# Attention sums of a graph network kernel: numerators scaled from SBUF, small products in one PSUM bank and earlier in TensorE's order, six banks of sums added four tiles late

## What is computed

```python
h = (x @ W).reshape(num_nodes, H, C)
a_src = (h * att_src).sum(-1)
a_dst = (h * att_dst).sum(-1)
e = jax.nn.leaky_relu(a_src[src] + a_dst[dst], NEG_SLOPE)
m = jax.ops.segment_max(e, dst, num_segments=num_nodes)
ex = jnp.exp(e - m[dst])
denom = jax.ops.segment_sum(ex, dst, num_segments=num_nodes)
alpha = ex / denom[dst]
out = jax.ops.segment_sum(alpha[:, :, None] * h[src], dst, num_segments=num_nodes)
```

## Time and profile before

| | |
|---|---|
| median of 3 runs | 11274.33 us (11269.1 to 11277.22) |
| span of the profiled execution | 11269.5 us |
| first attention sum, first to last tile on TensorE | 6399.8 to 7944.4 us |
| second attention sum | 8037.7 to 9565.7 us |
| busy share of the span | PE 66%, DVE 54%, ACT 29%, POOL 59% |

### The profile page before, as it was taken

How to read it: one execution, slowest core, us unless ns; L and a number is a source line. 1 busy time by engine, 2 the same in 40 slices (tenths; PEclk the granted TensorE clock), 3 DMA queues, 4 the chain that set the end, 5 groups by cost and what they waited for, 6 DMA issues and landing times. The chain is left out here.

```text
span 11269.5 us, 163779 instructions
## 1 busy us (share of the span) xinstructions
PE 7444.9 (66%) x37173; PEld 5482.0 (49%) x37173; DVE 6117.7 (54%) x21451; ACT 3221.2 (29%) x10474; POOL 6628.6 (59%) x7026
## 2 busy tenths in 40 slices
PE   4444444443466677578888666677577677788888
PEld 3222223333324555434434455556566566777777
DVE  5555544333324555455544466566566666677777
ACT  1111110000011111000000244444344444677776
POOL 4666666666644666656666466666466664555554
PEclk5566655555568888655555566666666666999999
DMA  3222223111143111111111122222122221211111
GB/s 89 69 77 77 72 79 80 46 46 46 44 163 128 44 44 44 44 48 45 46 46 46 45 48 48 48 48 49 44 48 49 49 49 38 79 41 41 41 41 40
DMA packets 297939, 639.01 MB, mean 57 GB/s; under 512 B 125149, under 2 KB 165984, under 8 KB 285534
## 3 DMA queue, kind: packets, MB, share of 16 engines
q0 software_dynamic: 223872, 420.21, 15.3%
q1 hardware_dynamic: 73470, 212.61, 5.6%
HBM read 479.52 MB, written 152.84 MB: 56 GB/s over the span
## 5 line engine op out<-in xcount | busy, mean ns | idle before, releaser
L1313 POOL DMA_INDIRECT relsum_rows<-relation_table,tab_idx x1870 | 1764.0, 943 | 1176.4 <-issue 463.6
L1364 PE MATMUL relsum_sums<-relsum_hot,relsum_rows 128*128 128x128 f32 x3740 | 950.2, 399 | 1055.2 <-issue 513.2
L1364 PEld LDWEIGHTS relsum_sums<-relsum_hot,relsum_rows 128*128 128x128 f32 x3740 | 782.6, 268 | 1274.5 <-issue 1239.1
L1097 POOL DMA_INDIRECT conv_rows<-tensor_table,src_idx x997 | 939.9, 943 | 754.3 <-PE conv_sums L2482 352.1
L1097 POOL DMA_INDIRECT gat1sum_rows<-gat_table,src_idx x997 | 941.2, 944 | 600.5 <-PE gat1sum_sums L2093 277.6
L1097 POOL DMA_INDIRECT gat2sum_rows<-gat_table,src_idx x997 | 942.2, 945 | 587.8 <-PE gat2sum_sums L2093 307.1
L1313 POOL DMA_INDIRECT gcnsum_rows<-x_table,src_idx x997 | 943.8, 947 | 553.2 <-issue 247.0
L727 POOL DMA_INDIRECT records<-sort_recs,place_rows x968 | 926.8, 957 | 581.5 <-DVE place_rows L234 303.7
L1323 DVE TENSOR_SCALAR relsum_hot<-relsum_digits,dst_rel,w 128x128 f32<-128x128 f32 x1994 | 803.3, 403 | 411.4 <-issue 410.8
L2091 PE MATMUL gat1sum_sums<-gat1sum_hot,gat1sum_scaled 128*128 128x128 f32 x1994 | 678.5, 439 | 421.8 <-DVE gat1sum_scaled L2020 367.0
L2091 PE MATMUL gat2sum_sums<-gat2sum_hot,gat2sum_scaled 128*128 128x128 f32 x1994 | 668.3, 434 | 426.2 <-DVE gat2sum_scaled L2020 300.5
(11 more groups left out here) (436 smaller groups left out, 16112.1 us busy)
## 6 DMA issues: line engine op xcount, KB each, us to landing
relation_table<-table_row SPq DMA_DIRECT2D x30, 2048.0 KB
relation_table<-sort_space SPq DMA_DIRECT2D x40, 1024.0 KB
place_lo_wide<-lo_rows SPq DMA_DIRECT2D x121, 256.0 KB
relsum_rows<-relation_table,tab_idx POOLq DMA_INDIRECT x1870
relation_table<-place_extra SPq DMA_DIRECT2D x20, 1024.0 KB
gcnsum_rows<-x_table,src_idx POOLq DMA_INDIRECT x997
gat1sum_rows<-gat_table,src_idx POOLq DMA_INDIRECT x997
gat2sum_rows<-gat_table,src_idx POOLq DMA_INDIRECT x997
```

What stands on the lines that cost most here:

```text
L1097: pool.indirect_dma_start(bufs[:, t % depth, :], None, table, bass.IndirectOffsetOnAxis(ap=idx[:, t:t + 1], axis=0)).then_inc(landed[t % l ...
L1313: pool.indirect_dma_start(rows[:, t % depth, :], None, table, bass.IndirectOffsetOnAxis(ap=idx[:, t:t + 1], axis=0)).then_inc(landed[t % d ...
L1364: mm = pe.matmul(bank[:, 0:P], part, hot[:, t % HOTS, :], start=k == 0, stop=k == len(tile_rows) - 1)
```

## The change

`LEAD` = 4 and `LANES` = 6 are new. The sums get six banks, and VectorE adds the sums of the tile four before, where it was two before; `scaled` has six buffers; the list of window starts is padded by 4. The numerators are transposed into the bank of the small products, not into three banks of their own, and VectorE scales rows from the SBUF copy `p_col`, which now has three copies. On TensorE the fold moves from tile 6 to tile 3, the spread from 8 to 5, the numerators from 12 to 9, and the transposes of the scores from tile 0, for the next group, to tile 12, for the group after the next. Group 1 is transposed ahead of the first tile.

```diff
+LEAD = 4
+LANES = 6
...
-        p_col = sb("p_col", [P, P], F32)
+        p_col = sb("p_col", [P, PHASES, P], F32)
...
-        scaled = sb("scaled", [P, 4, HEADS, CH], F32)
+        scaled = sb("scaled", [P, LANES, HEADS, CH], F32)
...
-        p_ps = [ps(f"p{f}", [P, 512], F32) for f in range(PHASES)]
         small_ps = ps("small", [P, 512], F32)
         fold_ps, spread_ps, factor_ps = (small_ps[:, k * SLOT_BUFS:(k + 1) * SLOT_BUFS] for k in range(3))
-        sums = [ps(f"sums{j}", [P, 2, 256], F32) for j in range(3)]
+        p_ps = small_ps[:, P:2 * P]
+        sums = [ps(f"sums{j}", [P, 2, 256], F32) for j in range(LANES)]
...
-                act.copy(p_col[:, :], p_ps[f][:, 0:P])
+                act.copy(p_col[:, f, :], p_ps)
...
-            for j in range(3):
-                dve.memset(sums[j][:, :, :], 0.0)
-            dve.sem_inc(s["kept"], 1)
-            dve.drain().then_inc(s["added"], 1)
+            for bank in sums:
+                dve.memset(bank[:, :, :], 0.0)
+            dve.drain().then_inc(s["added"], LANES - LEAD)
...
-                dve.wait_ge(s["multiplied"], tile + v["multiplied"](held - 1))
-                dve.wait_ge(s["added"], tile + v["added"](1))
-                before, bank = (buf - 2) % held, sums[(buf - 2) % 3]
+                dve.wait_ge(s["multiplied"], tile + v["multiplied"](held - LEAD + 1))
+                dve.wait_ge(s["added"], tile + v["added"](LANES - LEAD))
+                before, bank = (buf - LEAD) % held, sums[(buf - LEAD) % LANES]
...
-                    tile, j, buf = g * SLOT_BUFS + k, k % 4, f * SLOT_BUFS + k
-                    dve.tensor_tensor(scaled[:, j, :, :], rows[:, buf, 0:D].rearrange("p (h c) -> p h c", h=HEADS),
-                                      over_columns(p_ps[f][:, k * HEADS:(k + 1) * HEADS], CH),
+                    tile, buf = g * SLOT_BUFS + k, f * SLOT_BUFS + k
+                    dve.tensor_tensor(scaled[:, buf % LANES, :, :], rows[:, buf, 0:D].rearrange("p (h c) -> p h c", h=HEADS),
+                                      over_columns(p_col[:, f, k * HEADS:(k + 1) * HEADS], CH),
                                       ALU.mult).then_inc(s["scaled_ready"], 1)
...
             turn_numerators(0, 0)
+            turn_scores(1, 1)
...
-                    elif k == 0:
-                        turn_scores(g + 1, next_f)
-                    elif k == 6:
+                    elif k == 3:
                         fold_ends(g + 1)
-                    elif k == 8:
+                    elif k == 5:
                         spread_chain(g + 1)
-                    elif k == 12:
+                    elif k == 9:
                         turn_numerators(g + 1, next_f)
+                    elif k == 12 and (not isinstance(g, int) or g + 2 < USED_GRPS):
+                        turn_scores(g + 2, (f + 2) % PHASES)
```

More of the change, by code:

```diff
@@ L931, in take @@
         dve.tensor_copy(self.dst[:, own], rec[:, :, R_DST]).then_inc(s["dst_ready"], 1)
-        dve.tensor_copy(env.win[:, 2 + own.start:2 + own.stop], rec[0:1, :, R_DST])
+        dve.tensor_copy(env.win[:, LEAD + own.start:LEAD + own.stop], rec[0:1, :, R_DST])
         dve.tensor_copy(env.src_idx[:, own], rec[:, :, R_SRC])
@@ L1104, in window_starts @@
     return env.nc.values_load_multi_w_load_instructions(
-        env.win[0:1, bass.ds(g * SLOT_BUFS + (2 - late), SLOT_BUFS)], engines=[DVE_ENGINE], min_val=0, max_val=N,
+        env.win[0:1, bass.ds(g * SLOT_BUFS + (LEAD - late), SLOT_BUFS)], engines=[DVE_ENGINE], min_val=0, max_val=N,
         skip_runtime_bounds_check_because="sorted destinations are node numbers")[1]
@@ L1887, in keep_numerators @@
                     act.copy(p_wide[:, f, 4 * turn:4 * turn + 4, :].rearrange("p k (h c) -> p (k h) c", c=CH),
-                             over_columns(p_col[:, 4 * turn * HEADS:4 * (turn + 1) * HEADS], CH)).then_inc(s["wide_ready"], 1)
+                             over_columns(p_col[:, f, 4 * turn * HEADS:4 * (turn + 1) * HEADS], CH)).then_inc(s["wide_ready"], 1)
             def build(g, turn):
@@ L2015, in group @@
             def group(g, f, last=False):
-                starts = window_starts(env, g, late=2)
+                starts = window_starts(env, g, late=LEAD)
                 dve.wait_ge(s["p_ready"], g + v["p_ready"](1))
                 for k in range(tiles_of(g)):
-                    tile, j, buf = g * SLOT_BUFS + k, k % 4, f * SLOT_BUFS + k
-                    dve.tensor_tensor(scaled[:, j, :, :], rows[:, buf, 0:D].rearrange("p (h c) -> p h c", h=HEADS),
-                                      over_columns(p_ps[f][:, k * HEADS:(k + 1) * HEADS], CH),
+                    tile, buf = g * SLOT_BUFS + k, f * SLOT_BUFS + k
+                    dve.tensor_tensor(scaled[:, buf % LANES, :, :], rows[:, buf, 0:D].rearrange("p (h c) -> p h c", h=HEADS),
+                                      over_columns(p_col[:, f, k * HEADS:(k + 1) * HEADS], CH),
                                       ALU.mult).then_inc(s["scaled_ready"], 1)
@@ L2026, in group @@
                 if last:
-                    for k in range(tiles_of(g), tiles_of(g) + 2):
+                    for k in range(tiles_of(g), tiles_of(g) + LEAD):
                         add(g * SLOT_BUFS + k, f * SLOT_BUFS + k, starts[k])
@@ L2074, in group @@
                 for k in range(tiles_of(g)):
-                    tile, j, bank = g * SLOT_BUFS + k, k % 4, sums[(f * SLOT_BUFS + k) % 3]
+                    tile, lane = g * SLOT_BUFS + k, (f * SLOT_BUFS + k) % LANES
+                    bank = sums[lane]
                     if last:
                         pass
-                    elif k == 0:
-                        turn_scores(g + 1, next_f)
-                    elif k == 6:
+                    elif k == 3:
                         fold_ends(g + 1)
-                    elif k == 8:
+                    elif k == 5:
                         spread_chain(g + 1)
-                    elif k == 12:
+                    elif k == 9:
                         turn_numerators(g + 1, next_f)
+                    elif k == 12 and (not isinstance(g, int) or g + 2 < USED_GRPS):
+                        turn_scores(g + 2, (f + 2) % PHASES)
                     if k % 4 == 0:
@@ L2090, in group @@
                     pe.wait_ge(s["added"], tile + v["added"](1))
-                    pe.matmul(bank[:, 0, 0:P], scaled[:, j, :, :].rearrange("p h c -> p (h c)"), hot[:, k, :], start=True,
+                    pe.matmul(bank[:, 0, 0:P], scaled[:, lane, :, :].rearrange("p h c -> p (h c)"), hot[:, k, :], start=True,
                               stop=True)
@@ L2106, in attend @@
                          ("wide_ready", turns), ("dist_ready", 4 * USED_GRPS - 2), ("hot_ready", 16 * USED_GRPS - 8),
-                         ("scaled_ready", USED), ("multiplied", USED + held), ("added", USED + 3)):
+                         ("scaled_ready", USED), ("multiplied", USED + held), ("added", USED + LANES)):
             sig[n].passed(count)
@@ L2632, in build @@
         env.dst_rel = env.keep("dst_rel", [P, TILES + SLOT_BUFS], F32)
-        env.win = env.keep("win", [1, 2 + TILES], I32)
+        env.win = env.keep("win", [1, LEAD + TILES], I32)
         small_tensors(env)
```

6 lines of the change are left out of this document (3 added, 3 removed).

## The result

The changed kernel takes 11357.69 us (median of 4 runs, 11349.39 to 11363.39) against 11275.19 us for the kernel before beside it: ratio 1.0071, 95% interval 1.0058 to 1.0085. Forecast were 10,872 us, 402 us less; it came out 82 us more.

A forecast was written before the change was run, and what follows sets the result against it. It took late TensorE answers, with three tiles sharing one round trip, to bound the attention sums. Terms -155 - 42 - 43 + 35 + 1 + 3 = -201 us a sum, -402 for two, gave 10,872 us, range 10,680 to 11,120.

The forecast's parts named there:

- the edit touches two of its stages: Starting premise: only the two attention sums are edited, so only they were read; no size given for other stages.
- no change: Rival: the 1.57 us pace is already TensorE's progress and only waits change hands; 11,274 us, chance 0.05.
- Six banks, sums added 4 tiles late: Attention sums: two thirds of VectorE's 231 us of waits at the additions go, -155 us a sum.
- the lags are in TensorE's own progress: Rival, attention sums: more banks don't help beyond 1.46 us a tile; -110 and -92 us, 11,072 us, chance 0.22.
- The account of the pace by a round trip shared by 3 tiles: Attention sums: 4.7 us of product, 2.6 us lag, add and scaling per 3 tiles, 1.57 us each.
- Small products earlier: Attention sums: VectorE's softmax waits shrink by 42 and 43 us a sum; a TensorE hold at tile 9 adds 35.
- Slower: three round trips a group: Rival, attention sums: TensorE and VectorE wait for each other at three steps; +321 us, 11,595 us, chance 0.08.
- Numerators from SBUF: Attention sums: 997 scalings read SBUF instead of PSUM at 1 ns more each, +1 us a sum.
- The slower case in which scaling and gathers collide: Rival, attention sums: each scaling waits 0.28 us on gathers, 558 us in all; 11,430 us, chance 0.03.
- What stays: Attention sums: 132.2 us of waits at group heads untouched; extra clears and additions taken as 3 us a sum.
- My sign of being wrong: Attention sums: L1965, L1970 and L2010 wait as long as before, or L2020's mean rises past 0.4 us.

The follow-up runs named there:

- e1: Kernel before with only the window-start table padded by two more words, so each group of 16 is read 8 bytes later: ratio 1.0146, 11301.17 us.
- e14: The changed kernel as it stands, run again on a chip where the kernel before takes 11,136 us: ratio 1.0074.
- e15: Changed kernel with fold, spread and numerators at tiles 5, 7, 11, scores at 12, and aligned window loads in the convolution: ratio 0.9924 against the kernel before.
- e4: Changed kernel with TensorE's small steps back at tiles 0, 6, 8 and 12: ratio 1.0012 against the kernel before.
- e13: The kernel before, unchanged, one run beside e14 to e16 on a chip where it takes 11,136 us.
- e16: Changed kernel with TensorE's old order, aligned convolution loads and the attention sums' loops written out: ratio 0.9890 against the kernel before.
- e2: Changed kernel with 40 one-column memsets ahead of VectorE's convolution loop: ratio 1.0074 against the kernel before.
- e7: Changed kernel with three banks, adds 2 tiles late and the window table as before, new TensorE order kept: ratio 1.0756 against the kernel before.
- e8: As e7 but with TensorE's old order too: ratio 1.0009 against the kernel before.
- e5: The kernel before, unchanged, one run on the chip where it takes 9,274 us.
- e6: Changed kernel whose convolution first copies the window table so its loads are aligned: ratio 1.0064 against the kernel before, on the 9,274 us chip.
- e12: Same kernel as e16, on a chip where the kernel before takes 9,274 us: ratio 1.0000, 9,273 us.

## Why the prediction was wrong

The sum left out a term (+92 and -37 us), took one large term six times too big (-155 us a sum, measured about -25) and had another with the wrong sign (-50 us a sum, measured +42 and +26).

*Not in the sum: the loads of window starts.* The step that failed is "the edit touches two of its stages": nothing in the prediction speaks of where the 16 words begin. The rows were in the trace: 3.60 us a load in the relational and graph sums, 1.10 in the others, in the same kernel before. 63 groups with 2.5 us more are 158 us of VectorE in the convolution, of which 92 show; 189 groups with 2.5 us less are some 470 us in the three other sums, of which 37 show. That VectorE isn't what these mostly wait for would explain it, but was not tried. That alone turns "no change" into 0.5% slower, and e1, e14 and e15 show it.

*"Six banks, sums added 4 tiles late", -155 us a sum.* The wait was rightly read but the step from a shorter wait to a shorter stage failed. In e4 the wait at the additions fell from 248.3 to 78.4 us, more than I forecast, and the waits for the small products rose by 64 us. Against e13, on a chip of the same speed, the additions wait 180 us less (258.1 to 78.4), the small products 109 us more (102.7 to 211.3, the rows that name a transfer and those that name TensorE) and the heads of groups 28 us more. The six banks with the old order are worth some 25 us a stage: e4's sums take 1496.1 and 1488.0 us, e13's 1521.3 and 1512.5, on two chips whose kernels before agree within 2 us. By e4's own ratio it is the same: 14 us above before, of which 92 are the convolution's, -37 and 8 the rest as in e14, leaves -49 for both sums.

I read this so: what VectorE waits for is TensorE, whichever product it asks for. That comes nearest to the rival "the lags are in TensorE's own progress", but it is argued and not shown, for TensorE in its turn waits for VectorE's rows (200.7 us in e4). The rival's pace of 1.46 us a tile isn't reached even with the loops written out: in e16 the tiles with gathers take 1420.5 and 1424.8 us, 1.50 a tile. It named 110 and 92 us of gain; with the loops it is 26 and 25 (e15), 54 and 41 without. The account of the pace by a round trip shared by 3 tiles, 1.57 us, fitted a lag chosen between two cases; with 5 tiles sharing it the same sum would give 0.94 us and leave the pace to the gathers' 1.25, while e4's tiles with gathers take 1.53. The match with 1.57 came of the choice of the lag.

*"Small products earlier", -42 - 43 + 35 = -50 us a sum.* L1941's wait did go, and those of L1965 and L1970, 86.1 us, came to 33 us at L1967 and L1972. But I priced a hold at tile 9 only, and the dearest is that at tile 3, where TensorE stands with its tiles behind it: 191 us. The step as a whole costs 42 and 26 us (e2 against e4) in place of giving 50. With six banks it takes back what they gave, and that makes the two attention sums 15 us longer (e14) where the sum had 402 less. "Slower: three round trips a group" was this mechanism; it stands plainly where the adds are 2 tiles late (e7, +366 and +319 us over e8, 5.9 and 5.2 us a group for the 9 that it named), and in the change itself the slack of 4 tiles hides most of it. I gave it 0.08 because I worked out each from the kernel before and not the second with the first in place.

*"Numerators from SBUF", +1 us.* Measured +6 and +5 (e8 against e5), at the edge of what one profile each can tell; the rows show 6 ns on each of 997 scalings. The slower case in which scaling and gathers collide did not occur: 286 ns on the mean.

*"What stays".* The jumps back every 48 tiles were 5.0 us on the mean in the first sum and 3.8 in the second, against 0.83 us at the other heads. By e16 against e15 they cost 28 and 16 us. Nor did they stay: in the changed kernel's first sum they are 6.0 us (20 passes, 20 us more), in e7 and e8 3.9 and 4.0, and in the second sum 3.8 to 4.0 in every variant with a loop and loads of 1.10 us. What moves them stays open.

Right were: L1941's wait, that TensorE stands ahead of its small products (3.3 us at a time at the fold, where I wrote less than 2), scalings under 0.3 us. GpSimd's waits for TensorE were to fall to near 100 us and stayed at 285.1. My sign of being wrong, that L1965, L1970 and L2010 wait as long as before, came for L2010 alone, and its reason (work of TensorE that no buffer hides) doesn't follow: e4 shows that buffers do shorten that wait.

## What to carry to other kernels

When a change moves a table or a buffer's first word, look up who else reads it, and from which byte: the stage that lost the time was not in the diff's subject. Before a small product is moved up in an in-order engine's program, compare the tile at which it is asked for with the tile at which its input is made; what stands behind it is held for the difference, and slack won elsewhere is used up by it. And read a wait's cure by where the next wait of the same engine is: in e4 the additions wait 180 us less than in e13, and the stage is 25 us shorter.

## What the runs showed of the hardware

- A load of 16 words into VectorE's registers takes 1.10 us where it starts a multiple of 16 bytes from the table's first word (16g and 16g + 4 words) and 3.60 us where it starts 8 bytes off that (16g + 2), by the medians of every stage looked at (e1, e5, e6, e14). Offsets of 4 or 12 bytes weren't tried, and where the table itself begins no view shows.
- The same program takes 9,274 us on one chip and 11,136 on another. VectorE's and GpSimd's instructions take the same time (an addition 414 ns, gathers 1.25 us at their closest). TensorE's don't in the attention sums: in the first the median durations of a tile's two products are 421 and 421 ns in e13 and 377 and 275 in e5, where the granted clock is 0.64 and 0.80 on the mean. Whether the lower clock there is cause or effect of the slower pace no run told. Beside e5's row above, e13's:
```profile
6345.20:7866.50 1521.30, 1067.16 (x4669) 903.72 (x4668) 937.91 (x3981) 715.80 (x2282) 908.15 (x961) 0.64 0.20 47
```
The clock alone isn't the difference, as the graph sum shows: there it is 0.51 on both, nearly all of it at the lower of the two levels (1.2 GHz of 1.2 and 2.4), and the stage takes 1445.3 and 1243.7 us. GpSimd's groups there, e13 and e5:
```profile
L1313 POOL DMA_INDIRECT gcnsum_rows<-x_table,src_idx x997 | 944.6, 947 | 539.5 <-issue 256.9 <-PE gcnsum_sums L1364 205.9 <-SPq L1273 46.0
```
```profile
L1313 POOL DMA_INDIRECT gcnsum_rows<-x_table,src_idx x997 | 951.5, 954 | 333.2 <-issue 165.7 <-PE gcnsum_sums L1364 137.7 <-SPq L1273 29.8
```
In e13 there are 77 stretches of over 1 us in that stage in which no instruction starts on any engine, 107 us in all; in e5 there is none. Of the trace's records of the counter that TensorE raises for each tile of the first attention sum, 170 of 857 come within 0.1 us of the one before in e13, none of 967 in e5, while products are 1.25 us apart. So on the one chip completions are recorded late and in bunches. I take these to be the lags of the earlier trace rows. The traces with them also hold a third as many records of counters as the others (49,543 in the first, 147,330 in e5). What delays the completions, and whether recording them has a part in it, stays open; no run told it apart.
- At the head of the convolution's loop, which jumps back every 16 tiles, VectorE is idle for 0.98 us with aligned loads, 1.10 us of load partly under the addition before it. At the head of the attention sums' loops, every 48 tiles, it is idle for 3.8 to 6.1 us, and the longer program without loops has about 1 us there (e16; 1.5 in e12). That fits the rule of the Trainium skill ("Runtime: NRT & Kernel Launch", Instruction fetch mechanics) that a jump to a block of instructions no longer held waits for a fetch; no run here varied the length of a loop.
